# Weight transposes woven into the first chunk's projections, and a narrower wait in the attention loop

## The chip, the cores and the metric

One Trainium2 chip, all 8 cores. Every core runs the same program on its own batch entry (8 entries); the cores exchange nothing. The metric is device microseconds of the slowest core.

## What is computed

For each batch entry x (4096 x 2048, float32), with layernorms that have no weights:

```
q, k, v = LN(x) @ wq.T, LN(x) @ wk.T, LN(x) @ wv.T      # 16 heads of 128, q scaled by 1/sqrt(128)
scores  = einsum('bshd,bstd->bsht', q, k)               # at each position, its 16 heads against each other
out     = softmax(scores) @ v                           # then transposed and reshaped to 4096 x 2048
x = x + LN(out @ wo.T)
ternary(w) = clip(round(w / mean|w|), -1, 1)            # for w1, w2 (5632 x 2048), w3 (2048 x 5632)
x = x + LN((sigmoid(h @ ternary(w1).T) * (h @ ternary(w2).T)) @ ternary(w3).T),   h = LN(x)
```

All weights arrive as float32 with the wrong axis on the partitions, so each is cast (or made ternary) to bf16 and transposed 128 x 128 at a time on TensorE against an identity. The transposed copy is written to HBM and streamed from there.

## The kernel before

The program is one list of instructions for each engine, filled by Python in the order of the code. Each engine works its own list strictly in order. Counters T, V and C count what TensorE (PE), VectorE (DVE) and ScalarE (ACT) have finished. `emit` puts the waits in front of an instruction; `dma` puts a transfer on the list of the engine named (SyncE "sync"/SP, ScalarE "scalar"/ACT, GpSimd "gpsimd"/POOL), so the transfer is not issued before that engine has come to it, and each engine's transfers use four semaphore slots in turn.

**Prelude.** 64 weight tiles (`units`: q, k, v, o, 16 row blocks of 128 each). Per tile: two loads of 128 x 1024 float32 (line 506; the first from SP, the second from POOL; four landing buffers `fwl`), two casts on DVE (line 511) into one of three `wstream` buffers, four groups of four 128 x 128 transposes on PE (line 523) into PSUM banks 2 and 3 in turn, a copy of each group on ACT (line 531) into one of three `tpstage` buffers, and a store of each group from ACT (line 535; for o line 540). A `tpstage` buffer is taken again when its store has landed. `wst_cons[b]` holds the T count at which `wstream[b]` was last read.

**Phase 2, eight chunks of 512 positions (c = 0..7).** Each chunk has:

- projections: 48 steps (q, k, v by 16 heads; gi = 0..47). A step loads one 128 x 2048 bf16 strip from SP (line 619) into `wstream[gi % 3]`, waiting for `wst_cons[gi % 3]`; runs 16 matmuls of 512 columns (line 626) into bank gi % 2; scatters the result on ACT (line 637 for q, 644 for k, 651 for v); and calls `emit_prep_step()`.
- the transpose of V: 16 groups (PE line 664, DVE line 669), a call of `emit_prep_step()` after each.
- the layernorm of the next chunk.
- the attention loop, lines 681 to 785: `a5_stage_a(it)` (scores on PE, maxima on DVE, line 696) and `a5_stage_b(it - 1)` (exponentials on ACT, line 713; reciprocals and a diagonal on DVE, lines 720 and 725; two rounds of matmuls, lines 734 and 749; copies on ACT, line 742, and DVE, line 767), eight iterations with two halves hv each. `emit_prep_light()` is called at the end of each stage b. In iterations 3 and 7 ACT stores half of the chunk's result.

`emit_prep_step()` does one step of the preparation of w1, w2, w3: first the 272 tiles for the means ("gamma", two to a step, so 136 steps; loads from POOL and ACT in turn, line 359, absolute sums on DVE, line 368), then three steps that compute the thresholds, then 272 "quant" steps (one load from POOL, two DVE instructions, two groups of transposes, copies on ACT, line 454, stores from ACT, line 460). `emit_prep_light()` does gamma only. When gamma is done, the light calls do nothing.

After the eight chunks come the output projection and the feed-forward part, which need `woT`, `w1T`, `w2T` and `w3T`.

Of the kernel before, what the change touches and what calls it, by code (L numbers as in the profile page):

```python
# [29 lines left out]
def latest(toks):  # L30
    d = {}
    for c, v in toks:
        k = id(c)
        if k not in d or d[k][1] < v:
            d[k] = (c, v)
    return list(d.values())
# [37 lines left out]
def build_nc(debug=False):  # L74
# [82 lines left out]
    T = _mkctr("T", 1)  # L157
    V = _mkctr("V", 1)
# [38 lines left out]
    def se(waits, build, inc=None):  # L197
        emit("scalar", waits, build, inc)
# [5 lines left out]
    def dma(eng, waits, build):  # L204
        q = QENG[eng]
        slot = q.next_slot()
        emit(eng, list(waits) + [(slot, slot.n)], build, inc=slot, fresh=True)
        return (slot, slot.n)
# [204 lines left out]
    def emit_quant_step():  # L413
        if q_state["i"] >= len(q_tiles):
            return False
        wi, srcw, t, c0, cw = q_tiles[q_state["i"]]
        if not thr_state["done"][wi]:
            return False
        b = q_state["i"] % 2
        q_state["i"] += 1  # L420
        tok = dma("gpsimd", [(V, q_state["cons"][b])],
                  lambda e, d=wload_q[b], s=srcw, t=t, c0=c0, cw=cw:
                  e.dma_start(d[:, 0:cw],
                              s[t * 128:(t + 1) * 128, c0:c0 + cw]))
        fg = q_state["first_gate"]
        q_state["first_gate"] = []
        ve([tok, (V, thr_state["v"][wi])] + fg,
           lambda e, s=wload_q[b], cw=cw, wi=wi: e.tensor_scalar(  # L428
               lbuf[:, 0:cw], s[:, 0:cw], thrn[:, wi:wi + 1], None,
               ALU.is_le), V)  # L430
        ve([(T, q_state["mm"][b])],
           lambda e, s=wload_q[b], q=qstage[b], cw=cw, wi=wi:
           e.scalar_tensor_tensor(q[:, 0:cw], s[:, 0:cw],  # L433
                                  thr[:, wi:wi + 1], lbuf[:, 0:cw],
                                  ALU.is_ge, ALU.subtract), V)
        q_state["cons"][b] = V.n
        stt_v = V.n
        for g in range(cw // 512):
            bank = 2 + q_state["tp"] % 2
            tb = q_state["tp"] % 3  # L440
            q_state["tp"] += 1
            tw = [(V, stt_v)] + (bank_free[bank] or []) + consts_toks
            for i in range(4):
                te(tw if i == 0 else [],
                   lambda e, bk=bank, q=qstage[b], g=g, i=i: e.matmul(  # L445
                       ps[bk][:, i * 128:(i + 1) * 128],
                       q[:, g * 512 + i * 128: g * 512 + (i + 1) * 128],
                       ident, start=True, stop=True),
                   T if i == 3 else None)
            mm = T.n  # L450
            q_state["mm"][b] = mm
            se([(T, mm)] + ([q_state["tp_cons"][tb]]
                            if q_state["tp_cons"][tb] else []),
               lambda e, bk=bank, tb=tb: e.copy(tpstage[tb], ps[bk][:]), C)  # L454
            bank_free[bank] = [(C, C.n)]
            if wi < 2:
                wTd = w1T_h if wi == 0 else w2T_h
                stok = dma("scalar", [(C, C.n)],
                           lambda e, d=wTd, t=t, c0=c0, g=g, tb=tb:
                           e.dma_start(  # L460
                               d[t][:, c0 + g * 512: c0 + (g + 1) * 512],
                               tpstage[tb]))
            else:
                ccb = (c0 + g * 512) // 128
                zoff = (t % 4) * 128
                stok = dma(
                    "scalar", [(C, C.n)],
                    lambda e, t=t, ccb=ccb, zoff=zoff, tb=tb: e.dma_start(
                        w3T_h[t // 4].rearrange("p (cc z) -> p cc z", z=512)[
                            :, ccb:ccb + 4, zoff:zoff + 128],  # L470
                        tpstage[tb].rearrange("p (i z) -> p i z", i=4)))
            q_state["tp_cons"][tb] = stok
            q_state["store_toks"][wi].append(stok)
        return True
# [19 lines left out]
    fwl_cons = [0, 0, 0, 0]  # L494
    fwl_toks = []
    wst_cons = [0, 0, 0]
    wT_gate = {w: {} for w in ("q", "k", "v", "o")}
    units = [(w, t) for w in ("q", "k", "v", "o") for t in range(16)]
    for u, (w, t) in enumerate(units):
        cb_ = u % 3  # L500
        src = win["w" + w] if w != "o" else win["wo"]
        for hf in range(2):
            fb = (2 * u + hf) % 4
            ltok = dma("sync" if hf == 0 else "gpsimd",
                       [(V, fwl_cons[fb])],
                       lambda e, d=fwl[fb], s=src, t=t, hf=hf: e.dma_start(
                           d, s[t * 128:(t + 1) * 128,
                                hf * 1024:(hf + 1) * 1024]))
            fwl_toks.append(ltok)
            ve([ltok, (T, wst_cons[cb_])],  # L510
               lambda e, d=wstream[cb_], s=fwl[fb], hf=hf: e.tensor_copy(
                   d[:, hf * 1024:(hf + 1) * 1024], s), V)
            fwl_cons[fb] = V.n
        cast_v = V.n
        toks = []
        for g in range(4):
            bank = 2 + g % 2
            tb = q_state["tp"] % 3
            q_state["tp"] += 1
            tw = [(V, cast_v)] + (bank_free[bank] or []) + consts_toks  # L520
            for i in range(4):
                te(tw if i == 0 else [],
                   lambda e, bk=bank, s=wstream[cb_], g=g, i=i: e.matmul(  # L523
                       ps[bk][:, i * 128:(i + 1) * 128],
                       s[:, (g * 4 + i) * 128:(g * 4 + i + 1) * 128],
                       ident, start=True, stop=True),
                   T if i == 3 else None)
            mm = T.n
            se([(T, mm)] + ([q_state["tp_cons"][tb]]
                            if q_state["tp_cons"][tb] else []),  # L530
               lambda e, bk=bank, tb=tb: e.copy(tpstage[tb], ps[bk][:]), C)  # L531
            bank_free[bank] = [(C, C.n)]
            if w != "o":
                stok = dma("scalar", [(C, C.n)],
                           lambda e, w=w, t=t, g=g, tb=tb: e.dma_start(
                               wT[w][t][:, g * 512:(g + 1) * 512],
                               tpstage[tb]))
            else:
                stok = dma("scalar", [(C, C.n)],
                           lambda e, t=t, g=g, tb=tb: e.dma_start(  # L540
                               woT_h[4 * g:4 * g + 4][
                                   :, :, t * 128:(t + 1) * 128].rearrange(
                                   "j p c -> p j c"),
                               tpstage[tb].rearrange("p (j c) -> p j c",
                                                     j=4)))
            q_state["tp_cons"][tb] = stok
            toks.append(stok)
        wst_cons[cb_] = T.n
        wT_gate[w][t] = toks
    woT_gate = latest([t for h in range(16) for t in wT_gate["o"][h]])  # L550
    fwl_gate = latest(fwl_toks)
    fcmax = max(fwl_cons)
    q_state["cons"] = [fcmax, fcmax]
    q_state["first_gate"] = fwl_gate

    if NPHASES <= 1:
        ops_end(nc, refs, ops, Q_S, Q_C, Q_G, se, emit)
# [5 lines left out]
    A_half_tok = [[None, None] for _ in range(NCH)]  # L563
    last_exp = [0, 0]
    last_rec = [0, 0]
    nmx_v = [0, 0]
    last_aT_mm = [0, 0]
    last_out_mm = [0, 0]
    ln1T_ready = [None, None]
# [39 lines left out]
    for c in range(NCH):  # L609
# [3 lines left out]
        for pi, p in enumerate(("q", "k", "v")):  # L613
            ename = "scalar"
            for h in range(H):
# [35 lines left out]
                       lambda e, d=dst, s=srcp: e.activation(d, s, ACT.Copy),  # L651
                       C)
                bank_free[bank] = [(ECTR[ename], ECTR[ename].n)]
                emit_prep_step()
        ln1T_cons[par] = T.n
        qkv_done = [(V, V.n), (C, C.n)]

# [20 lines left out]
        def a5_stage_a(it):  # L678
            for hv in range(2):
# [5 lines left out]
                for i in range(4):  # L685
# [10 lines left out]
                   lambda e, b=sbk, d=nm: e.tensor_reduce(  # L696
                       d, ps[b][:].rearrange("p (g cc) -> p g cc", g=4),
                       AX.X, ALU.max, negate=True), V)
                nmx_v[hv] = V.n

        def a5_stage_b(it):
            nonlocal_A = [0]
            for hv in range(2):
# [3 lines left out]
                ex = expS[hv]  # L707
                su = sums4[hv]
                for g in range(4):
                    se([(V, nmx_v[hv]), (T, last_aT_mm[hv]),  # L710
                        (V, last_rec[hv])] if g == 0 else [],
                       lambda e, b=sbk, g=g, ex=ex, nm=nm, su=su:
                       e.activation(ex[:, g * 128:(g + 1) * 128],  # L713
                                    ps[b][:, g * 128:(g + 1) * 128],
                                    ACT.Exp, bias=nm[:, g:g + 1],
                                    accum_out=su[:, g:g + 1]), C)
# [76 lines left out]
    w1T_gate = latest(q_state["store_toks"][0])  # L793
    w2T_gate = latest(q_state["store_toks"][1])
    w3T_gate = latest(q_state["store_toks"][2])

    if NPHASES <= 2:
        ops_end(nc, refs, ops, Q_S, Q_C, Q_G, se, emit)
# [404 lines left out]
```

How the kernel before makes its waits and increments, by code:

```python
        def step(e, ws=ws, build=build, inc=inc):  # L180
            for ctr, val in ws:
                e.wait_ge(ctr.sem, val)
            ins = build(e)
            if inc is not None:
                if ins is None:
                    e.nop().then_inc(inc.sem, inc.step)
                else:
                    ins.then_inc(inc.sem, inc.step)
```

## Time and profile before

| what | us |
| --- | --- |
| median of 5 runs | 10075.22 |
| lowest and highest of them | 9974.32, 10541.44 |
| the profiled execution | 9962.73 |
| its span on core 7, the slowest, read below | 9960.8 |
| spans of the 8 cores in it | 9795.2 to 9960.8 |

A stretch of the trace is given by its start and end in us from the start of the span. The chunks of core 7 were told apart by the first and last start of the matmuls of lines 626, 664 and 749: chunk 0's projections run from 577.0, chunk 1's from 1049.9, chunk 2's from 1480.7, chunk 4's from 2418.9, chunk 6's from 3339.8, chunk 7's from 3672.5, and the output projection begins at 3968.4. PE is busy for 67% of the span, and the other engines for a quarter or less.

### The profile page before, as it was taken

What the parts mean: (1) busy time and instruction counts of PE and PEld (TensorE: products, weight loads), DVE (VectorE), ACT (ScalarE), POOL (GpSimd) and SP (SyncE); (2) the same over time, 40 slices, a digit from 0 to 9 for tenths busy, and PEclk for the clock granted to TensorE, in tenths of its full rate; (3) what the DMA queues carried; (4) which work ended last, traced back from release to release, by engine and by line L of the source; (5) the groups of instructions that cost most, each with busy time, mean ns of one, the idle gap of its engine ahead of it and who ended that gap; (6) DMA issues with size and microseconds to landing.
All of it is one profiled execution on the core that took longest, in us unless ns stands there. A gap on an engine that the chain in (4) does not pass through costs nothing.

```text
span 9960.8 us, 102628 instructions; the slowest of 8 cores (9795.2 to 9960.8 us)
## 1 busy us (share of the span) xinstructions
PE 6637.0 (67%) x30924; PEld 2992.5 (30%) x30924; DVE 2522.0 (25%) x3692; ACT 1956.5 (20%) x3811; POOL 414.7 (4%) x764
## 2 busy tenths in 40 slices
PE   2253637374645666686786786886885885896896
PEld 1121213232323323232332332332332332332342
DVE  1146554444444321202102102102102102102101
ACT  2231224334343442101001001001001001001000
POOL 0000001010000000000000000000000000000000
PEclk9996859586867777798898998998997897786787
DMA  7777858484757532343443443443443443442433
GB/s 210 200 242 222 259 166 248 120 243 132 229 150 206 146 109 87 116 148 113 138 144 108 145 150 104 151 148 103 149 143 99 153 141 99 137 144 93 142 121 108
DMA packets 725709, 1510.76 MB, mean 152 GB/s; under 512 B 316336, under 2 KB 418992, under 8 KB 704688
## 3 DMA queue, kind: packets, MB, share of 16 engines
q1 hardware_dynamic: 300464, 772.17, 24.9%
q10 hardware_dynamic: 340864, 421.61, 13.7%
q0 software_dynamic: 83840, 310.43, 11.0%
q8 instruction: 259, 4.24, 0.2%
q14 instruction: 282, 2.31, 0.1%
HBM read 1283.75 MB, written 203.42 MB: 149 GB/s over the span
## 4 chain that ended last, share of the span: by engine, by line
PE 44%; DMA 26%; DVE 13%; ACT 9%; issue 6%; ACTq 1%; DVEq 1%; SPq 0%; POOLq 0%
PE ps L981 12%; PE ps L990 12%; PE ps L1037 9%; DMA bfar<-w3T 6%; PE ps L626 5%; DMA bfar<-woT 4%; DMA f32ar<-w 4%; PE ps L880 2%; ACT bfar L713 2%; DMA w1T<-bfar 2%; DMA w3T<-bfar 2%; ACT bfar L454 2%; DVE f32ar L368 1%; DVE f32ar L273 1%; DMA w2T<-bfar 1%
## 5 line engine op out<-in xcount | busy, mean ns | idle before, releaser
L1037 PE MATMUL ps<-bfar 128*128 128x512 bf16 x5632 | 1365.8, 405 | 661.6 <-DMA bfar<-w3T 661.2
L626 PE MATMUL ps<-bfar 128*128 128x512 bf16 x6144 | 1437.2, 392 | 160.7 <-DMA bfar<-wT_q 67.5
L981 PE MATMUL ps<-bfar 128*128 128x512 bf16 x5632 | 1357.0, 397 | 232.5 <-ACT f32ar L1000 199.5
L990 PE MATMUL ps<-bfar 128*128 128x512 bf16 x5632 | 1327.9, 391 | 0.0
L1037 PEld LDWEIGHTS ps<-bfar 128*128 128x128 bf16 x5632 | 564.4, 103 | 1459.5 <-issue 1023.5
L626 PEld LDWEIGHTS ps<-bfar 128*128 128x128 bf16 x6144 | 602.4, 100 | 902.1 <-issue 281.2
L981 PEld LDWEIGHTS ps<-bfar 128*128 128x128 bf16 x5632 | 569.0, 101 | 965.6 <-issue 455.5
L1006 DVE TENSOR_TENSOR bfar<-ps,f32ar 128x512 bf16<-128x512 f32 x352 | 243.4, 691 | 2244.6 <-PE ps L990 2222.8
L990 PEld LDWEIGHTS ps<-bfar 128*128 128x128 bf16 x5632 | 563.7, 100 | 706.0 <-issue 178.1
L880 PE MATMUL ps<-bfar 128*128 128x512 bf16 x2048 | 566.5, 427 | 272.8 <-DMA bfar<-woT 223.4
L1000 ACT ACTIVATE f32ar<-ps 128x512 f32<-128x512 f32 x352 | 210.2, 597 | 2210.0 <-PE ps L981 2209.3
L734 PE MATMUL ps<-bfar 128*128 128x128 bf16 x512 | 75.0, 301 | 645.3 <-DVE bfar L725 645.3
L1062 DVE TENSOR_REDUCE f32ar<-bfar 128x1 f32<-128x512 bf16 x128 | 87.8, 686 | 1596.7 <-ACT bfar L1055 1590.1
L445 PE MATMUL ps<-bfar 128*128 128x128 bf16 x2112 | 208.0, 240 | 371.7 <-DVE bfar L433 218.7
L454 ACT CAST bfar<-ps 128x512 bf16<-128x512 f32 x528 | 309.5, 586 | 663.0 <-PE ps L445 300.1
L523 PE MATMUL ps<-bfar 128*128 128x128 bf16 x1024 | 149.7, 300 | 367.7 <-ACT bfar L531 353.2
L880 PEld LDWEIGHTS ps<-bfar 128*128 128x128 bf16 x2048 | 203.4, 105 | 635.6 <-issue 505.7
L368 DVE TENSOR_REDUCE f32ar<-f32ar 128x1 f32<-128x1024 f32 (+1 forms) x269 | 319.6, 1188 | 258.1 <-DMA f32ar<-w 242.6
L433 DVE SCALAR_TENSOR_TENSOR bfar<-bfar,f32ar 128x1024 bf16<-128x1024 f32 (+1 forms) x272 | 340.9, 1253 | 95.6 <-PE ps L445 71.3
L637 ACT ACTIVATE bfar<-ps,f32ar 128x512 bf16<-128x512 f32 x128 | 312.8, 2444 | 225.1 <-PE ps L626 102.9
L1055 ACT CAST bfar<-ps 128x512 bf16<-128x512 f32 x64 | 37.5, 586 | 1550.8 <-PE ps L1037 1548.1
L428 DVE TENSOR_SCALAR bfar<-bfar,f32ar 128x1024 f32<-128x1024 f32 (+1 forms) x272 | 200.7, 738 | 517.0 <-DMA bfar<-w 507.9
(100 smaller groups left out, 3801.5 us busy)
## 6 DMA issues: line engine op xcount, KB each, us to landing
bfar<-w1T SPq DMA_DIRECT2D x352, 512.0 KB, 3.6
bfar<-w2T SPq DMA_DIRECT2D x352, 512.0 KB, 3.7
bfar<-w POOLq DMA_DIRECT2D x256, 512.0 KB, 6.1
bfar<-w3T ACTq DMA_DIRECT2D x192, 512.0 KB
bfar<-w3T SPq DMA_DIRECT2D x160, 512.0 KB, 3.6
f32ar<-w POOLq DMA_DIRECT2D x136, 512.0 KB, 6.7
bfar<-wT_q SPq DMA_DIRECT2D x128, 512.0 KB, 5.6
bfar<-wT_k SPq DMA_DIRECT2D x128, 512.0 KB, 6.4
```

Source lines behind the costliest of these rows:

```text
L368: ve([tok], lambda e, s=wload_g[b], cw=cw, a=acol: e.tensor_reduce(gtmp[:, a + 8:a + 9], s[:, 0:cw], AX.X, ALU.add, apply_absolute_value=T ...
L433: e.scalar_tensor_tensor(q[:, 0:cw], s[:, 0:cw], thr[:, wi:wi + 1], lbuf[:, 0:cw], ALU.is_ge, ALU.subtract), V)
L445: lambda e, bk=bank, q=qstage[b], g=g, i=i: e.matmul(ps[bk][:, i * 128:(i + 1) * 128], q[:, g * 512 + i * 128: g * 512 + (i + 1) * 128], i ...
L454: lambda e, bk=bank, tb=tb: e.copy(tpstage[tb], ps[bk][:]), C)
L626: e.matmul(ps[b][:], wl[:, Dc * 128:(Dc + 1) * 128], lt[:, Dc * 512:(Dc + 1) * 512], start=(Dc == 0), stop=(Dc == 15)),
L637: lambda e, d=dst, s=srcp: e.activation(d, s, ACT.Copy, scale=c_qs), C)
L880: te(tw, lambda e, cbq=cbq, sl=sl, j=j: e.matmul(ps[cbq][:], Aslab[cbq][:, j * 128:(j + 1) * 128], wostrip[sl], start=(j == 0), stop=(j == ...
L981: lambda e, b=b1, s1=s1, lt=lt, Dc=Dc: e.matmul(ps[b][:], wpool[s1][:, Dc * 128:(Dc + 1) * 128], lt[:, Dc * 512:(Dc + 1) * 512], start=(Dc ...
L990: lambda e, b=b2, s2=s2, lt=lt, Dc=Dc: e.matmul(ps[b][:], wpool[s2][:, Dc * 128:(Dc + 1) * 128], lt[:, Dc * 512:(Dc + 1) * 512], start=(Dc ...
L1000: lambda e, b=b1, sg=sg: e.activation(sg, ps[b][:], ACT.Sigmoid), C)
L1006: ve(mw, lambda e, b=b2, cp=cp, sg=sg: e.tensor_tensor(hid[:, cp * 512:(cp + 1) * 512], ps[b][:], sg, ALU.mult), V)
L1037: posb=posb: e.matmul(ps[b][:], hid[:, cc * 512 + posb * 128: cc * 512 + (posb + 1) * 128], wpool[sl][:, ccl * 512:(ccl + 1) * 512], start ...
```

## The change

The prelude keeps its first 16 tiles (q). The body of the prelude's loop becomes `emit_wunit_step()`. The other 48 tiles (k, v, o) are emitted one by one in chunk 0's projections, in place of that chunk's 48 calls of `emit_prep_step()`, each behind the step's scatter. For these 48, the two loads are issued from POOL and ACT instead of SP and POOL. The tile u still goes into `wstream[u % 3]`. What depended on all 64 tiles (first use of the quant buffers, `woT_gate`) is computed where it is needed. In the attention loop, `nmx_v` gets four entries instead of two, so that the exponentials of iteration it wait for the maxima of iteration it, not for those of it + 1.

```diff
--- before.py
+++ after.py
@@ -416,6 +416,11 @@
         wi, srcw, t, c0, cw = q_tiles[q_state["i"]]
         if not thr_state["done"][wi]:
             return False
+        if q_state["i"] == 0:
+            assert wunit_state["i"] == len(units)
+            fcmax = max(fwl_cons)
+            q_state["cons"] = [fcmax, fcmax]
+            q_state["first_gate"] = latest(fwl_toks)
         b = q_state["i"] % 2
         q_state["i"] += 1
         tok = dma("gpsimd", [(V, q_state["cons"][b])],
@@ -496,13 +501,21 @@
     wst_cons = [0, 0, 0]
     wT_gate = {w: {} for w in ("q", "k", "v", "o")}
     units = [(w, t) for w in ("q", "k", "v", "o") for t in range(16)]
-    for u, (w, t) in enumerate(units):
+    wunit_state = {"i": 0}
+
+    def emit_wunit_step():
+        u = wunit_state["i"]
+        if u >= len(units):
+            return False
+        wunit_state["i"] += 1
+        w, t = units[u]
+        woven = u >= 16
         cb_ = u % 3
-        src = win["w" + w] if w != "o" else win["wo"]
+        src = win["w" + w]
         for hf in range(2):
             fb = (2 * u + hf) % 4
-            ltok = dma("sync" if hf == 0 else "gpsimd",
-                       [(V, fwl_cons[fb])],
+            eng = (("gpsimd", "scalar") if woven else ("sync", "gpsimd"))[hf]
+            ltok = dma(eng, [(V, fwl_cons[fb])],
                        lambda e, d=fwl[fb], s=src, t=t, hf=hf: e.dma_start(
                            d, s[t * 128:(t + 1) * 128,
                                 hf * 1024:(hf + 1) * 1024]))
@@ -547,11 +560,10 @@
             toks.append(stok)
         wst_cons[cb_] = T.n
         wT_gate[w][t] = toks
-    woT_gate = latest([t for h in range(16) for t in wT_gate["o"][h]])
-    fwl_gate = latest(fwl_toks)
-    fcmax = max(fwl_cons)
-    q_state["cons"] = [fcmax, fcmax]
-    q_state["first_gate"] = fwl_gate
+        return True
+
+    for _ in range(16):
+        emit_wunit_step()
 
     if NPHASES <= 1:
         ops_end(nc, refs, ops, Q_S, Q_C, Q_G, se, emit)
@@ -563,7 +575,7 @@
     A_half_tok = [[None, None] for _ in range(NCH)]
     last_exp = [0, 0]
     last_rec = [0, 0]
-    nmx_v = [0, 0]
+    nmx_v = [0, 0, 0, 0]
     last_aT_mm = [0, 0]
     last_out_mm = [0, 0]
     ln1T_ready = [None, None]
@@ -651,7 +663,10 @@
                        lambda e, d=dst, s=srcp: e.activation(d, s, ACT.Copy),
                        C)
                 bank_free[bank] = [(ECTR[ename], ECTR[ename].n)]
-                emit_prep_step()
+                if c == 0:
+                    emit_wunit_step()
+                else:
+                    emit_prep_step()
         ln1T_cons[par] = T.n
         qkv_done = [(V, V.n), (C, C.n)]
 
@@ -696,7 +711,7 @@
                    lambda e, b=sbk, d=nm: e.tensor_reduce(
                        d, ps[b][:].rearrange("p (g cc) -> p g cc", g=4),
                        AX.X, ALU.max, negate=True), V)
-                nmx_v[hv] = V.n
+                nmx_v[2 * (it % 2) + hv] = V.n
 
         def a5_stage_b(it):
             nonlocal_A = [0]
@@ -707,7 +722,7 @@
                 ex = expS[hv]
                 su = sums4[hv]
                 for g in range(4):
-                    se([(V, nmx_v[hv]), (T, last_aT_mm[hv]),
+                    se([(V, nmx_v[2 * (it % 2) + hv]), (T, last_aT_mm[hv]),
                         (V, last_rec[hv])] if g == 0 else [],
                        lambda e, b=sbk, g=g, ex=ex, nm=nm, su=su:
                        e.activation(ex[:, g * 128:(g + 1) * 128],
@@ -793,6 +808,7 @@
     w1T_gate = latest(q_state["store_toks"][0])
     w2T_gate = latest(q_state["store_toks"][1])
     w3T_gate = latest(q_state["store_toks"][2])
+    woT_gate = latest([t for h in range(16) for t in wT_gate["o"][h]])
 
     if NPHASES <= 2:
         ops_end(nc, refs, ops, Q_S, Q_C, Q_G, se, emit)
```

## Rows read from the trace of the kernel before

**Rows 1.** The page: busy us (share) xcount of each engine; the chain by engine

```profile
PE 6637.0 (67%) x30924; PEld 2992.5 (30%) x30924; DVE 2522.0 (25%) x3692; ACT 1956.5 (20%) x3811; POOL 414.7 (4%) x764
...
PE 44%; DMA 26%; DVE 13%; ACT 9%; issue 6%; ACTq 1%; DVEq 1%; SPq 0%; POOLq 0%
```

**Rows 2.** Stretches, core 7: start:end, length, busy us (count), granted clock, DMA share, GB/s

```profile
137.40:517.00 379.60, 112.39 (x771) 66.80 (x770) 66.25 (x94) 112.55 (x192) 24.24 (x46) 1.00 0.75 197
...
576.90:813.30 236.40, 184.11 (x768) 75.47 (x768) 117.20 (x170) 56.65 (x46) 22.17 (x42) 0.96 0.94 299
...
931.20:1049.80 118.60, 28.17 (x184) 17.66 (x184) 53.40 (x100) 36.33 (x135) 3.69 (x7) 0.50 0.37 99
...
1049.80:1276.80 227.00, 178.97 (x770) 74.46 (x768) 118.45 (x178) 56.64 (x46) 23.22 (x44) 0.96 0.97 315
...
1389.80:1480.60 90.80, 28.18 (x184) 17.66 (x184) 34.09 (x72) 36.32 (x135) 0.00 (x0) 0.50 0.19 48
...
1727.50:1817.00 89.50, 24.14 (x184) 17.08 (x184) 40.94 (x45) 17.58 (x30) 7.91 (x15) 0.51 0.44 129
...
2418.80:2664.00 245.20, 203.27 (x1146) 99.12 (x1145) 98.64 (x98) 112.98 (x141) 26.14 (x48) 0.94 0.89 261
...
2418.80:2885.90 467.10, 260.48 (x1546) 136.91 (x1544) 193.58 (x236) 187.81 (x374) 34.61 (x64) 0.74 0.64 183
...
3339.70:3672.50 332.80, 219.30 (x1177) 107.65 (x1176) 100.31 (x146) 133.93 (x282) 9.39 (x17) 0.79 0.49 146
...
3533.90:3546.30 12.40, 7.70 (x64) 4.80 (x64) 10.22 (x15) 3.19 (x11) 0.00 (x0) 0.70 0.00 0
...
3672.50:3839.90 167.40, 167.37 (x770) 75.41 (x768) 0.85 (x2) 57.35 (x47) 0.00 (x0) 0.99 0.45 148
```

**Rows 3.** In order of time (start, us), core 7: a weight tile of the prelude

```profile
138.00 1.49 DVE L511 CAST bfar<-bfar 128x1024 bf16<-128x1024 f32 x2 [7.96 <-PE ps L523]
...
138.90 0.59 ACT L531 CAST bfar<-ps 128x512 bf16<-128x512 f32 x1 [0.61 <-ACT bfar L531]
...
139.62 0.33 ACTq L535 DMA_DIRECT2D wT_q<-bfar  x1
...
139.63 0.58 PE L523 MATMUL ps<-bfar 128*128 128x128 bf16 x4 [0.61 <-ACT bfar L531]
...
140.09 0.59 ACT L531 CAST bfar<-ps 128x512 bf16<-128x512 f32 x1 [0.61 <-DMA wT_q<-bfar]
```

**Rows 4.** In order of time, core 7, chunk 0's projections

```profile
583.64 2.43 ACT L637 ACTIVATE bfar<-ps,f32ar 128x512 bf16<-128x512 f32 x1 [37.40 <-PE ps L626]
...
586.14 0.35 ACTq L359 DMA_DIRECT2D f32ar<-w  x1
...
603.25 5.30 PE L626 MATMUL ps<-bfar 128*128 128x512 bf16 x16 [2.29 <-DMA bfar<-wT_q]
...
609.07 3.61 PE L626 MATMUL ps<-bfar 128*128 128x512 bf16 x16 [0.52 <-DMA bfar<-wT_q]
```

**Rows 5.** Transfers: line 506's and the last chunk's strips, us from issue to landing

```profile
DMA to landing us min/median/max: 4.1/6.3/13.1
...
bfar<-wT_k SPq DMA_DIRECT2D x16, 512.0 KB, 3.4
```

**Rows 6.** Line 644, the scatter of a K strip: forms, duration

```profile
L644 ACT ACTIVATE bfar<-ps x128: 597/597/598, 662.1 to 3784.8; 128x512 bf16<-128x512 f32 x128
```

**Rows 7.** In order of time, core 7, the attention loop of the last chunk

```profile
3891.78 0.59 ACT L742 CAST bfar<-ps 128x512 bf16<-128x512 f32 x1 [2.02 <-PE ps L734]
...
3894.33 1.49 DVE L696 TENSOR_REDUCE f32ar<-ps 128x4 f32<-128x512 f32 x2
...
3895.17 0.37 ACT L713 ACTIVATE bfar<-ps,f32ar 128x128 bf16<-128x128 f32 x1 [2.80 <-DVE f32ar L696]
...
3897.09 0.19 ACT L713 ACTIVATION_READ_ACCUMULATOR bfar<-ps,f32ar 128x1 f32 x1
...
3897.46 0.18 DVE L720 RECIPROCAL f32ar<-f32ar 128x4 f32<-128x4 f32 x1 [1.64 <-ACT bfar L713]
```

## The prediction

> **What bounds the kernel now.** I read the page first. Its chain of waits belongs to PE for 44%, to transfers for 26% and to DVE for 13% [rows 1], so no single engine is the limit, and each stage has to be read alone. The stretches of core 7 [rows 2] divide the part that the change touches:
>
> - The part of the prelude for the 48 tiles of k, v and o is 137.4 to 517.0, 379.6 us or 7.9 us a tile, with PE busy for 112 us (771 matmuls against 48 x 16 = 768) and the transfers for 75% of the time.
> - Chunk 0's projections take 236.4 us with transfers busy for 94% at 299 GB/s. The same 768 matmuls take 167.4 us in chunk 7, where nothing is woven in. So the gamma loads set chunk 0's pace: 4.9 us a step against 3.5.
> - Chunk 1's projections (gamma in each step) take 227.0 us, 4.73 a step. Chunk 4's (quant in each) take 245.2, 5.1 a step.
> - The attention loop takes 90.8 us without gamma (chunk 1) and 118.6 with it (chunk 0).
>
> The change takes 48 tiles out of a stage that does nothing else, and puts them under matmuls. The question is what one of the 48 steps costs afterwards.
>
> **Removed.** The prelude ends 379.6 us earlier. The layernorm of chunk 0 behind it is unchanged. Chunk 0's projections in their present form, 236.4 us, go too. Together -616.
>
> **Added: 48 steps of matmuls plus tile.** I follow the lists of the engines. At step gi, the strip is in `wstream[gi % 3]` and the tile u = 16 + gi goes into `wstream[(16 + gi) % 3]`, which is `wstream[(gi + 1) % 3]`: exactly the buffer of the next strip. The load of strip gi + 1 therefore waits until the tile's last transposes have read that buffer. Before, a strip was loaded up to two steps ahead; now none is. The second wait is on ACT: the tile's second load stands on ACT's list behind the scatter of step gi, which waits for the matmuls of step gi. So one step is a chain without overlap:
>
> - 16 matmuls. After an idle time of 2.29 us a group of 16 took 5.30 us, and one that PE entered after only 0.52 us took 3.61 [rows 4]. At the lower of the clock's two levels throughout (512 columns at 1.2 GHz are 0.427 us) it would be 6.8. The two waits of a step are longer than 2.29 us, so I take 6.6, near that end. Bounds: 3.6 and 7.0.
> - Scatter on ACT: 2.43 us for q [rows 4], 0.60 for k and v [rows 6]. With 0.15 for the hand-overs from PE and to the load's issue (586.07 to 586.14 is one of them, [rows 4]) 0.75, for q 2.6.
> - ACT's load of 512 KB. In the prelude such loads landed after 6.3 us in the median, 4.1 at least; strips of the same size in chunk 7, where the transfers are busy for 45% of the time, after 3.4 [rows 2, 5]. Here it shares the 16 transfer engines with little, so I take 3.7. Bounds 3.4 and 6.3.
> - The cast of that half: two took 1.49 us [rows 3], so 0.75, with hand-overs 0.95.
> - Four groups of transposes. PE needs 0.58 a group and starts the third and the fourth 0.14 us after ACT has copied the first and the second; ACT's copies are 1.2 us apart (0.59 for the copy, the rest the store's issue) [rows 3]. So 0.58 + 0.15 + 0.59 + 0.61 + 0.59 + 0.14 + 0.58 = 3.24. The fourth copy also waits for the first store, but PE does not need it, and the ACT list is free long before the next scatter.
> - The strip. It lands beside the tile's stores and POOL's load of a tile ahead, so I take 4.5 rather than 3.4 (bounds 3.4 and 6.3); with 0.2 for hand-overs 4.7.
>
> Sum for k and v: 6.6 + 0.75 + 3.7 + 0.95 + 3.24 + 4.7 = 19.9 us; for q 21.8. 16 x 21.8 + 32 x 19.94 = 987 us. Nothing hides it: PE's list has no other work in this stage. With all lower bounds a step is 15.5 (q 17.4): 775. With all upper bounds 24.7 (q 26.5): 1214.
>
> On the clock, the Trainium skill ("TensorE: Matmul & The Clock Gate", section "HAM oscillation — how this bites in real kernels") says that groups of matmuls with a wait for data between them fall back to the lower clock, each group anew. By that rule every one of the 48 groups would take 16 x 0.427 = 6.8, some 10 us more in all than I take. This trace agrees in kind: the stretches where PE waits often show a granted clock of 0.50, those with dense matmuls 0.94 to 0.99 [rows 2].
>
> **Moved: gamma.** 48 of its 136 steps are displaced. Counting calls (64 `prep_step` a chunk, 8 light): chunk 0 now does 24 gamma steps, chunk 1 72, chunk 2 the last 40, then 3 thresholds and 21 quant; chunks 3 to 5 64 each; 59 are left for chunk 6, which does 19 now. Chunk 7 stays free, so nothing spills behind the chunks.
>
> - Chunk 1's attention loop now carries gamma: 118.6 - 90.8 = +28.
> - Chunk 2: 40 steps at gamma's 4.73 instead of quant's 5.1: -15.
> - Chunk 6 becomes nearly a chunk 4 (467.1 us with 64 quant steps). Five steps fewer in the V transposes, at (89.5 - 12.4) / 16 = 4.8 each, make 443, against 332.8 now [rows 2]: +110.
>
> Together +123. Moving gamma out of chunk 0 is thus no gain; it is paid later, under matmuls that were partly free.
>
> **The narrower wait.** In the loop the exponentials of iteration it start at 3895.17, released by the first of two maxima of it + 1 that run from 3894.33 to 3895.82, though ACT had ended its last copy at 3892.37; they end at 3897.28, and the reciprocal starts at 3897.46 [rows 7]. With the new counts ACT starts about 3892.5 and ends about 3894.6. But the reciprocal stands behind both maxima on DVE's list, so it starts at 3895.9 at the earliest: 1.5 us gained, not 2.7. The last iteration has no later maxima, and the one behind the store in iteration 3 waits on ACT for that store. Six of eight gain: 6 x 1.5 x 8 chunks = 74 us. Bounds: 0 (the store's wait or gamma behind the loop takes it) and 2.7 x 7 x 8 = 151.
>
> **Sum.** 9962.7 - 616 + 987 + 123 - 74 = 10,383, that is +420 on the profiled execution. That execution is 112 us below the median of the runs shown, and I add the +420 to that median: 10,490 us, rounded.
>
> **Rivals.**
>
> - *Hidden after all (the other side).* If strips and the second load were still prefetched, a step would cost PE's own 6.6 + 3.24 = 9.8 at most, or with a warm clock the 7.9 of a prelude tile: 48 x 7.9 = 379, and the sum is 9,775 (9,887 on the median). It decides below (616 - 123 + 74) / 48 = 11.8 us a step. For it: PE and transfers together would have room. Against it: the buffer numbers and the place on ACT's list are in the code, and my lowest step is 15.5. Chance 0.06.
> - *Only one wait is real.* If ACT's load were early, a step would be 6.6 + 3.24 + 4.7 = 14.6, 698 us in all, and the sum 10,094 (+1.3%). Against it: ACT's list is in order, as the load at 586.14 right behind the scatter's end at 586.07 shows [rows 4]. If besides a wait were cheaper than the rows say, the result would be within 1%. Chance 0.08 for all of this, 0.05 of it within 1%.
> - *Transfers as slow as in the prelude.* A step is 24.7, all 1214 us, the sum 10,610, on the median 10,720. For it: the strip lands next to four stores, and those of o are in short pieces. Against it: the transfers would carry 2 MB in 20 us, 100 GB/s, against 197 in the prelude. Chance 0.10.
>
> **How the numbers follow.** The forecast (serial steps of 16 to 23 us) has 0.76, the slow transfers 0.10, one wait 0.08, hidden 0.06. Range: with the lower bounds of the steps the result is 212 us lower (10,280), with the upper ones 228 us higher (10,720); the profiled execution being 112 us under the median lowers the lower end a little. 10,230 to 10,730. A measurement of this kernel can hardly tell less than 1% from no change. Faster by over 1%: 0.06; within 1%: 0.05; slower by over 1%: 0.89.
>
> **What would show it.** In the new trace: 16 tiles of line 523's kind before chunk 0, whose projections begin near 197; then a stretch of some 990 us in which PE waits twice a step, once for a cast (its cause ACT's load) and once for the strip, with the granted clock near 0.5 and transfers near 100 GB/s; strips issued right after a tile's last transposes. Attention loops of 82 us rather than 90.8. Chunk 6 about 110 us longer, the feed-forward part unchanged. I am wrong if strips are issued ahead, if a step is under 12 us, or if the displaced gamma costs nothing.

## The result, and the profile after

| | before | after |
| --- | --- | --- |
| median of all runs, us | 10263.66 (10 runs) | 10526.53 (6 runs) |
| the profiled execution, us | 9962.73 | 10371.89 |
| ratio, with its 95% interval | 1 | 1.0358 (1.0244 to 1.0473) |

The changed kernel is 3.6% slower. In some executions of either kernel the cores of one die or of both show a lower clock and take some per cent longer; the ratio and its interval leave these executions out, and the medians do not. The two profiled executions are 409 us apart.

The slowest core of the profile after is core 3 (before it was core 7). Its page divides the chain nearly as before [rows 1], so the page alone does not show where the time went.

```profile
PE 6684.7 (64%) x30924; PEld 3006.4 (29%) x30924; DVE 2523.1 (24%) x3692; ACT 1953.2 (19%) x3811; POOL 414.7 (4%) x764
...
PE 43%; DMA 28%; DVE 14%; ACT 8%; issue 6%; ACTq 1%; DVEq 1%; SPq 0%; POOLq 0%
```

The stretches show it. Columns as in [rows 2]: start:end, length, busy us of PE, PEld, DVE, ACT and POOL, granted clock, DMA share, GB/s. The rows are the q, k and v steps of chunk 0's projections, the attention loop of chunk 2, and chunk 6 whole.

```profile
195.40:538.30 342.90, 126.05 (x512) 55.48 (x512) 22.21 (x32) 74.88 (x79) 8.45 (x16) 0.63 0.30 94
538.30:867.10 328.80, 130.75 (x512) 56.41 (x512) 22.22 (x32) 47.05 (x81) 8.44 (x16) 0.58 0.34 103
867.10:1184.80 317.70, 128.09 (x495) 55.03 (x496) 20.82 (x30) 44.88 (x77) 7.90 (x15) 0.59 0.40 110
...
2241.70:2326.20 84.50, 28.85 (x189) 18.05 (x190) 34.22 (x73) 36.88 (x136) 0.00 (x0) 0.50 0.22 56
...
3703.80:4120.90 417.10, 250.31 (x1475) 129.30 (x1474) 177.03 (x226) 177.02 (x356) 31.07 (x57) 0.76 0.67 186
```

Chunk 0's projections now take 342.9 + 328.8 + 317.7 = 989.4 us, against 236.4, and neither PE (385 us busy) nor the transfers (a third of the time) are near a limit. That is a stage of waits. From the first matmul of one step to that of the next it is 21.7 us in the q steps and 20.5 in the k and v steps. One k step in order of time (core 3; the first column is the start, the second the duration):

```profile
646.65 5.94 PE L638 MATMUL ps<-bfar 128*128 128x512 bf16 x16 [5.23 <-DMA bfar<-wT_k]
652.68 0.60 ACT L656 ACTIVATE bfar<-ps 128x512 bf16<-128x512 f32 x1 [8.01 <-PE ps L638]
653.36 0.34 ACTq L519 DMA_DIRECT2D bfar<-wv  x1
657.68 1.49 DVE L524 CAST bfar<-bfar 128x1024 bf16<-128x1024 f32 x2 [18.96 <-DMA bfar<-wv]
658.63 1.01 PE L536 MATMUL ps<-bfar 128*128 128x128 bf16 x8 [6.05 <-DVE bfar L524]
...
661.29 0.59 PE L536 MATMUL ps<-bfar 128*128 128x128 bf16 x4 [0.61 <-ACT bfar L544]
...
662.21 0.32 SPq L631 DMA_DIRECT2D bfar<-wT_k  x1
...
666.76 6.12 PE L638 MATMUL ps<-bfar 128*128 128x512 bf16 x16 [4.89 <-DMA bfar<-wT_k]
```

Each link follows the one above it; between the two rows of transposes, and not shown, lie ACT's copies and the third group. PE waits twice: 6.05 us for the cast (line 524), which waits for the load that ACT could only issue at 653.36, behind its scatter; and 4.89 us for the strip, which SP issued at 662.21, when the tile's last transposes had ended at 661.88. The cast row holds two casts, this tile's second half and the next tile's first, whose load POOL had brought long before; PE goes on after the first of them.

### The profile page after: what moved, and what is told of

Same layout as the page of the kernel before. It is cut to its first block, busy times and chain, and to the rows that moved or that the text cites. A ratio compares the mean times of both kernels' runs of the same rounds, so it can differ in the third digit from the quotient of the medians.

```text
span 10370.3 us, 102724 instructions; the slowest of 8 cores (10232.5 to 10370.3 us)
## 1 busy us (share of the span) xinstructions
PE 6684.7 (64%) x30924; PEld 3006.4 (29%) x30924; DVE 2523.1 (24%) x3692; ACT 1953.2 (19%) x3811; POOL 414.7 (4%) x764
## 4 chain that ended last, share of the span: by engine, by line
PE 43%; DMA 28%; DVE 14%; ACT 8%; issue 6%; ACTq 1%; DVEq 1%; SPq 0%; POOLq 0%
PE ps L997 12%; PE ps L1006 11%; PE ps L1053 8%; DMA bfar<-w3T 6%; PE ps L638 6%; DMA bfar<-woT 4%; DMA f32ar<-w 4%; DMA w2T<-bfar 2%; PE ps L896 2%; DMA bfar<-w 2%; DVE f32ar L273 1%; DVE f32ar L368 1%; ACT bfar L728 1%; DVE bfar L438 1%; ACT bfar L459 1%
## 5 line engine op out<-in xcount | busy, mean ns | idle before, releaser
L459 ACT CAST bfar<-ps 128x512 bf16<-128x512 f32 x528 | 308.9, 585 | 707.9 <-PE ps L450 341.1
L524 DVE CAST bfar<-bfar 128x1024 bf16<-128x1024 f32 x128 | 88.8, 694 | 1055.8 <-DMA bfar<-wk 344.3
```

## The experiments

The ratios are to repeats of the kernel before that were run beside each kernel. Stage lengths are read from the trace of the core named, and where it is said so they are means over several cores. "Phase 2 ends" means the start of the last matmul of chunk 7's attention loop, counted from the start of the span. On the mean of the eight cores that is 3937 us in the kernel before and 4387 in the changed one.

### The tile in another buffer

```diff
-        cb_ = u % 3
+        cb_ = (u + 2) % 3 if woven else u % 3
```

> The changed kernel with one edit: a woven tile uses the wstream buffer of the strip that has just been multiplied, not that of the next strip. ACT still issues the tile's second load. Theory (a serial chain of two waits, in which the strip's load is one link): strips are again issued ahead, PE's wait for a strip goes, and a step of chunk 0 loses that link of about 4.9 us: 6.1 (matmuls) + 0.75 + 4.2 + 0.95 + 3.25 + 0.2 = 15.5 us for k and v, 17.3 for q, 773 us for the 48 steps against 989, so about 216 us less than the changed kernel. Rival (the transfers themselves, their sum or the ring of three staging buffers, set the 20.6 us): the stage stays within 5% of 989 us.

### The loads from SP and POOL

```diff
-            eng = (("gpsimd", "scalar") if woven else ("sync", "gpsimd"))[hf]
+            eng = ("sync", "gpsimd")[hf]
```

> The changed kernel with one edit: the woven tiles' loads are issued from SP and POOL, as in the prelude, so none stands behind the scatter on ACT. The buffer of the tile is still that of the next strip. Theory: scatter, ACT's load and the cast leave the chain: 6.1 + 3.25 + 4.9 + 0.2 = 14.4 us a step, the same for q as for k and v, 693 us for the stage, about 297 less than the changed kernel. Rival (transfers set the step): within 5% of 989 us. A second rival, that a load costs more on SP because SP waits there for the strip's buffer: between 693 and 989, with casts that wait for SP's load.

The stage rows of both, first the rotated buffer (core 1):

```profile
198.30:940.50 742.20, 352.04 (x1520) 164.82 (x1520) 65.23 (x94) 167.34 (x235) 25.31 (x48) 0.69 0.46 136
```

then the loads from SP and POOL (core 3):

```profile
192.80:870.00 677.20, 328.45 (x1520) 143.05 (x1521) 66.62 (x96) 167.02 (x235) 25.30 (x48) 0.73 0.49 150
```

989 became 742 us with the one edit (773 expected) and 677 with the other (693 expected). The means of the eight cores are 991, 740 and 675. The waits of PE in the stage, in us in total, times and longest, separate the two links. In the changed kernel (core 3) there are both kinds; the wait of 59.3 us in the q row is that for chunk 0's first strip, before the stage:

```profile
PE ps L536 <- DVE bfar L524: 304.2, 47, 7.7
...
PE ps L638 <- DMA bfar<-wT_q: 139.1, 16, 59.3
PE ps L638 <- DMA bfar<-wT_v: 85.0, 16, 7.7
PE ps L638 <- DMA bfar<-wT_k: 84.2, 16, 5.8
```

With the rotated buffer the wait for strips is gone but for the very first, and the wait for casts stays:

```profile
PE ps L536 <- DVE bfar L524: 338.8, 47, 14.4
...
PE ps L638 <- DMA bfar<-wT_q: 58.4, 1, 58.4
```

With the loads from SP and POOL it is the other way round: the wait for strips stays, and the one for casts no longer appears in the list:

```profile
PE ps L638 <- DMA bfar<-wT_q: 128.6, 16, 58.4
PE ps L638 <- DMA bfar<-wT_v: 80.9, 16, 6.3
PE ps L638 <- DMA bfar<-wT_k: 79.8, 16, 5.8
```

So each of the two edits of the code owns one wait, and both waits are needed for a step of some 21 us. The rival, that the transfers themselves set the pace, falls: the same transfers went through at 136 and 150 GB/s instead of about 100. The second rival of the SP loads, casts that wait for SP's load, falls too as far as PE is concerned, since PE waits for no cast.

### Both edits together

The two diffs above in one kernel.

> The changed kernel with both edits: the tile in the buffer of the strip just multiplied, and its loads from SP and POOL. Theory: no transfer is left in the chain; what remains is matmuls, two casts (the buffer is free only after the matmuls) and the transposes: 5.8 + 1.7 + 3.25 = 10.7 us at the lower clock level, 8.5 if the clock is at the upper one; I expect 9.5, 456 us for the stage, some 530 less than the changed kernel, which makes this kernel about 1% faster than the one before. Rival (transfers set the step): about 2 MB a step at the 299 GB/s that chunk 0 had before would be 7 us, so no limit here; if contention were the cause, the stage would stay above 700 us.

```profile
200.30:675.00 474.70, 295.21 (x1496) 135.13 (x1518) 66.20 (x96) 168.18 (x236) 25.31 (x48) 0.84 0.73 214
```

475 us (core 6), 456 expected. Single gains of 247 and 312 us add up to 559; together they gave 515. Against the kernel before the ratio is 0.9943 (0.9766 to 1.012), which by itself leaves open whether it is faster. The traces say that it is: phase 2 ends at 3852 us on the mean of the eight cores, 85 earlier than in the kernel before, and the part behind it is not changed by the edits. The granted clock of the stage rose from about 0.60 to 0.84, and PE is busy for 298 us (core 3, also a stage of 475 us) instead of 385 with the same matmuls. So 87 of the 515 us are the faster clock. It followed from the waits here, since nothing in these edits touches PE's work, but it is part of what removing them gave.

### Buffers of their own for the tiles

```diff
+    ubuf = [BF[:, 72832 + i * 2048: 72832 + (i + 1) * 2048]
+            for i in range(2)]
+    ub_cons = [0, 0]
...
-        cb_ = u % 3
+        cb_ = u % 2
...
-            ve([ltok, (T, wst_cons[cb_])],
-               lambda e, d=wstream[cb_], s=fwl[fb], hf=hf: e.tensor_copy(
+            ve([ltok, (T, ub_cons[cb_])],
+               lambda e, d=ubuf[cb_], s=fwl[fb], hf=hf: e.tensor_copy(
...
-                   lambda e, bk=bank, s=wstream[cb_], g=g, i=i: e.matmul(
+                   lambda e, bk=bank, s=ubuf[cb_], g=g, i=i: e.matmul(
...
-        wst_cons[cb_] = T.n
+        ub_cons[cb_] = T.n
...
-            eng = (("gpsimd", "scalar") if woven else ("sync", "gpsimd"))[hf]
+            eng = ("sync", "gpsimd")[hf]
```

> As the kernel with both edits, but the tiles have two buffers of their own in unused memory and leave wstream to the strips, so the casts run ahead too. Theory: a step is the larger of PE's own time (matmuls 3.5 to 5.8 plus transposes 3.25) and the 7.9 us that the ring of three staging buffers allows a tile: 8 to 9 us, about 405 us for the stage, 50 less than with the shared buffer, and 1.5 to 2% faster than the kernel before. Rival (the shared buffer was no limit once strips are early): no difference to the kernel with both edits.

```profile
192.90:665.10 472.20, 289.05 (x1519) 136.64 (x1520) 66.61 (x96) 167.27 (x235) 25.30 (x48) 0.83 0.76 215
```

472 us on core 3, where the mean of cores 0 to 3 is 465 and was 475 with both edits: 11 us less. I expected 405 us, so this is a miss, and the rival named there was nearly right. What took its place can be read from PE's waits before the transposes. With both edits (core 3, in the stage) PE waits for casts and for ACT's copies:

```profile
PE ps L536 <- DVE bfar L524: 85.4, 44, 2.3
PE ps L536 <- ACT bfar L544: 85.1, 96, 6.6
```

With own buffers (core 3) the wait for casts is gone from the list, and the wait for copies has grown by about as much:

```profile
PE ps L539 <- ACT bfar L547: 183.1, 119, 6.4
```

The copies in turn wait for staging buffers: ACT stands 165 us in the stage, 59 times, for stores to land (135 us with both edits; two rows of a k step, core 3):

```profile
413.12 0.59 ACT L547 CAST bfar<-ps 128x512 bf16<-128x512 f32 x1 [3.05 <-DMA wT_v<-bfar]
...
413.85 0.58 PE L539 MATMUL ps<-bfar 128*128 128x128 bf16 x4 [3.26 <-ACT bfar L547]
```

ACT stands 3.05 us for a store before it can copy a group, and PE, in order, waits 3.26 us behind it for the bank. Not every such wait costs PE its full length: one of 5.74 us at 406.45 lay under PE's matmuls and cost it 0.57. There is no ratio to the kernel before for this kernel. In the profiled execution cores 0 to 3 took 9691 to 9718 us, where those of the kernel before took 9795 to 9819.

### A longer ring

```diff
-    tpstage = [BF[:, 71808:72320], BF[:, 72320:72832], BF[:, 77952:78464]]
+    tpstage = [BF[:, 71808:72320], BF[:, 72320:72832], BF[:, 77952:78464],
+               BF[:, 76928:77440], BF[:, 77440:77952]]
...
-    Q_C = Queue("dC")
+    Q_C = Queue("dC", 8)
```

on top of the kernel with own buffers.

> The kernel with own buffers for the tiles and loads from SP and POOL, and besides five staging buffers instead of three and eight semaphore slots for ACT's transfers instead of four. Theory: the 7.9 us of a tile in the prelude are the round trip of a staging buffer (four groups over three buffers), so the 16 tiles that stay in the prelude take about 6.2 us each (-27 us), the woven steps about 7.5 (-25 to -60), quant steps may gain a little: 60 to 90 us less than with own buffers alone, about 2.5% faster than the kernel before. Rival (a tile is limited by the bandwidth, busy for 75%): no gain over the kernel with own buffers.

The prelude's 16 tiles without this edit, with it, and the stage with it (all core 3):

```profile
14.40:133.70 119.30, 35.95 (x248) 21.46 (x248) 22.26 (x31) 35.81 (x61) 7.92 (x15) 1.00 0.70 214
...
14.40:113.70 99.30, 36.07 (x248) 21.54 (x248) 21.87 (x30) 35.75 (x61) 7.92 (x15) 1.00 0.87 257
173.10:591.80 418.70, 268.86 (x1519) 131.47 (x1520) 66.60 (x96) 167.07 (x235) 25.32 (x48) 0.87 0.84 242
```

A tile of the prelude takes 99.3 / 16 = 6.2 us instead of 119.3 / 16 = 7.5, 20 us for the 16 tiles where 27 were expected. So the waits for stores were the limit, and the rival, a limit by bandwidth, falls: the same tiles moved at 257 GB/s instead of 214. The edit changes two things, the buffers and the semaphore slots, and they were not tried apart; with three buffers no more than three stores can be outstanding, so the four slots were not yet in the way.

The stage is 419 us, 53 less. ACT waits for stores 33 us instead of 165, and PE for copies 150 instead of 183. The rest is the clock: the same matmuls keep PE busy for 269 us instead of 289, at a granted clock of 0.87 instead of 0.83. On the mean of cores 0 to 3 phase 2 ends 95 us earlier than with own buffers alone (60 to 90 expected): 21 in the prelude, 52 in the stage, and the rest in later chunks, whose quant steps share the ring.

This kernel is faster than both: the ratio to the kernel before is 0.9767 (0.9632 to 0.9901), and its cores took 9591 to 9645 us in the profiled execution, where those of the changed kernel took 10233 to 10370. Of the 2.3%, 0.8% is the narrower wait (below). A q step still takes 9.9 us where a k step takes 7.3 (from the starts of their first matmuls), and the rows say why:

```profile
258.68 0.61 PE L541 MATMUL ps<-bfar 128*128 128x128 bf16 x8
258.94 2.40 ACT L654 ACTIVATE bfar<-ps,f32ar 128x512 bf16<-128x512 f32 x1 [3.37 <-PE ps L643]
...
261.42 0.59 ACT L549 CAST bfar<-ps 128x512 bf16<-128x512 f32 x1
...
262.15 0.38 PE L541 MATMUL ps<-bfar 128*128 128x128 bf16 x4 [2.86 <-ACT bfar L549]
...
263.57 5.30 PE L643 MATMUL ps<-bfar 128*128 128x512 bf16 x16
```

The copy that frees the third group's bank stands behind q's scatter of 2.40 us on ACT, PE waits 2.86 us for it, and the next 16 matmuls take 5.30 us, much as after the 2.29 us of idle time in [rows 4]. That four banks instead of two would remove this was not tried.

### The narrower wait alone

```diff
-    nmx_v = [0, 0]
+    nmx_v = [0, 0, 0, 0]
...
-                nmx_v[hv] = V.n
+                nmx_v[2 * (it % 2) + hv] = V.n
...
-                    se([(V, nmx_v[hv]), (T, last_aT_mm[hv]),
+                    se([(V, nmx_v[2 * (it % 2) + hv]), (T, last_aT_mm[hv]),
```

in the kernel before.

> The kernel before with only the narrower wait of the attention loop (four entries in nmx_v). Theory: the reciprocal stays behind the later maxima on DVE's list, so an iteration gains 1.5 us, not the 2.7 that ACT waited: attention loops of 82 instead of 90.6 us, with the first iteration's gain in front of them some 80 us in all, 0.8% faster. Rival (the whole wait is gained): loops of about 72 us, 150 us in all, 1.5% faster. Second rival (the gain is taken back by gamma or by the next chunk's layernorm): no change.

The attention loop of chunk 2 (core 1):

```profile
1816.00:1898.10 82.10, 28.01 (x183) 17.51 (x184) 34.10 (x72) 36.20 (x135) 0.00 (x0) 0.50 0.22 56
```

82.1 us, and 90.3 in the kernel before. From chunk 0's first projection to the last loop's end it is 3292 us (core 1) against 3373 on core 3 and 3376 on core 7 of the kernel before: 81 to 84 us less, 80 expected. The means of cores 0 to 3 are 3285 and 3365, also 80 less. The ratio is 0.9851 (0.9729 to 0.9974), faster, with a centre beyond what the trace accounts for but an interval that holds the 0.8%. Why the gain is 1.5 us an iteration and not 2.7 is to be seen in the changed kernel's loop (core 3, last chunk):

```profile
4314.63 0.58 ACT L757 CAST bfar<-ps 128x512 bf16<-128x512 f32 x1 [2.02 <-PE ps L749]
4315.31 0.37 ACT L728 ACTIVATE bfar<-ps,f32ar 128x128 bf16<-128x128 f32 x1
...
4317.18 1.49 DVE L711 TENSOR_REDUCE f32ar<-ps 128x4 f32<-128x512 f32 x2
...
4318.76 0.18 DVE L735 RECIPROCAL f32ar<-f32ar 128x4 f32<-128x4 f32 x1
```

ACT starts its exponentials at once and has ended them at 4317.41, but the reciprocal stands on DVE's list behind the maxima, which end at 4318.67. From the end of ACT's copy to the reciprocal it is 3.55 us; in [rows 7] it was 5.09. That is 1.54 us.

### The displaced gamma alone

```diff
-                emit_prep_step()
+                if c > 0:
+                    emit_prep_step()
```

in the projections of the kernel before.

> The kernel before, with its whole prelude, in which only chunk 0's projections call no preparation step; the 48 gamma steps move to later chunks, as in the changed kernel. Theory: chunk 0's projections fall from 236 to about 167 us (-69), and the displaced steps cost about +123 later (attention loop of chunk 1 +28, chunk 2 -15, chunk 6 +110): together +54 us, 0.5% slower. Rival (displaced work is absorbed in steps with room): -69 us, 0.7% faster.

Chunk 0's projections, chunk 0 whole, and the rest up to the end of the last attention loop (core 2):

```profile
566.30:734.20 167.90, 167.88 (x767) 75.66 (x768) 0.00 (x0) 57.31 (x47) 0.00 (x0) 1.00 0.45 157
566.30:956.50 390.20, 209.17 (x1040) 101.06 (x1040) 127.21 (x197) 113.38 (x248) 12.17 (x23) 0.72 0.48 152
956.50:3981.00 3024.50, 1707.23 (x9406) 857.14 (x9404) 1283.99 (x1747) 1087.93 (x2208) 205.04 (x383) 0.75 0.62 186
```

The same two stretches of the kernel before (core 7):

```profile
577.00:1049.90 472.90, 226.07 (x1041) 101.41 (x1042) 258.19 (x387) 113.31 (x248) 36.95 (x70) 0.74 0.74 231
1049.90:3953.20 2903.30, 1689.01 (x9405) 853.06 (x9404) 1151.79 (x1556) 1089.13 (x2208) 179.93 (x335) 0.75 0.59 176
```

Chunk 0 gains 83 us (69 of them in the projections, as expected; behind them the V transposes begin after 1.3 us and no longer after 18.7) and the later chunks pay 121. The net is +38 us between these two cores, +54 expected. The means of cores 0 to 3 of both kernels are 81 gained and 127 paid, a net of +46, and these cores took 9828 to 9873 us where those of the kernel before took 9795 to 9819. The rival, that displaced work disappears in steps with room, falls. There is no ratio for this kernel, so the size rests on the traces.

## Why the prediction was right

The prediction was 10,490 us, and the median is 10526.53. The sum made for the profiled execution was 10,383, and the profiled execution after took 10371.89. The mechanism, two waits that make a step serial, is shown by the first two experiments, and the size of every term by the traces. That the totals came out so close is partly luck, as the end of this section shows. Step by step, for a k step (the rows above):

| link | predicted | measured |
| --- | --- | --- |
| 16 matmuls, to the scatter's start | 6.6 + 0.08 | 652.68 - 646.65 = 6.03 |
| scatter, to the load's issue | 0.67 | 653.36 - 652.68 = 0.68 |
| ACT's load | 3.7 | 657.68 - 653.36 = 4.32 |
| cast | 0.95 | 658.63 - 657.68 = 0.95 |
| four groups of transposes | 3.24 | 661.88 - 658.63 = 3.25 |
| strip | 4.7 | 666.76 - 661.88 = 4.88 |
| step | 19.94 | 20.11 |

Two errors cancelled. The matmuls were 0.6 us faster than I took them, and the transfers slower by 0.6 and 0.2. Over the 48 groups the first and the last start lay 5.5 us apart on average on core 3 (5.6 on core 1), where the lower level throughout would make 15 x 0.427 = 6.4. In each of the 48 groups on core 3 the first two matmuls start 0.38 us apart and the next 0.43, which is the lower level, and the last two 0.22 to 0.26, which is the upper; 6 to 14 of the 15 intervals are long. The granted clock of the stage is accordingly 0.58 to 0.63, not near the 0.5 that I named.

The Trainium skill ("TensorE: Matmul & The Clock Gate", section "HAM oscillation — how this bites in real kernels") says that each group after a wait for data starts at the lower clock. This trace agrees: 48 of 48 groups started there. They did not stay there to their end, and my 6.6 us supposed that they nearly would.

The stage's 989.4 us end at the last step's matmuls. My 987 were for 48 whole steps, and these end with the last tile's transposes, 1002 us after the first matmul, when the transpose of V begins. The sum is hardly hurt, since what I took out, the old 236.4, was cut in the same way and had 18.7 us behind it where the new stage has 12.5.

Two readings in the prediction were not right, and neither moved the sum much. Six times 1.5 times 8 is 72; the 74 comes from an unrounded 1.54. And the sentence that stretches where PE waits often show a granted clock of 0.50 leaves out the prelude's row in [rows 2], which shows 1.00 with PE busy for 112 of 379.6 us. That 1.00 is not borne out by the matmuls: a group of four transposes takes 0.58 us there [rows 3], as it does in the k step above, and 0.38 in the stage of the kernel with the long ring. The trace of core 7 holds no record of the clock before 583.0 us, so the number says nothing about the prelude.

The terms, by the first matmul of each chunk, as means of the eight cores (chunk 7 up to the last matmul of its attention loop; the narrower wait is counted with 9 us a chunk; rounded):

| stretch | before | after | change | predicted |
| --- | --- | --- | --- | --- |
| up to chunk 0's projections | 564 | 195 | -369 | -380 |
| chunk 0's projections, first to last matmul | 236 | 991 | +756 | +751 |
| the rest of chunk 0 | 238 | 225 | -13 | -9 |
| chunk 1 | 431 | 465 | +34 | +19 |
| chunk 2 | 467 | 451 | -17 | -24 |
| chunks 3 to 5 | 1386 | 1373 | -13 | -28 |
| chunk 6 | 334 | 414 | +81 | +101 |
| chunk 7 | 282 | 272 | -10 | -9 |
| all | 3937 | 4387 | +450 | +421 |

- *Prelude.* Chunk 0's projections begin at 195 us. Before, they began at 577.0 on core 7, the core that I read, but at 564 on the mean of the cores and at 559 on core 3. So 382 us are gone by core 7, and 369 on average.
- *Narrower wait.* 80 us by the experiment alone, 74 predicted. Six of eight iterations gain, as I said: in the last chunk on core 3, counted by the first score matmuls, six are shorter by 1.5 to 1.8 us, the one behind the store by nothing (13.40 and 13.36 us), and the loop by 9.6 in all instead of the 9.2 that I took. In the changed kernel chunks 3 to 5 gained only 13 us together, where the experiment's gained 32 by the means of cores 0 to 3. Of the difference 10 us are the displaced gamma, which alone makes these three chunks 10 us longer. For the rest I have no cause; their projections also differ from core to core within one kernel (235.5 and 248.9 us in chunk 4 of the changed kernel, cores 0 and 3).
- *Displaced gamma.* 121 to 127 us by the experiment, 123 predicted. Inside the term there were two errors. Chunk 6 pays less: 417.1 us against 332.8, which with the 10 us of the narrower wait added back is +94, not +110. And chunk 1's projections, which I took to stay at 227.0, took 241.6 us in the changed kernel and 244 with the displaced gamma alone. The gamma tiles that chunk 1 reads are others than before: w3's tiles, one in six of them half as wide, had fallen into chunk 1 and now fall mostly into chunk 2. That accounts for a part only: the stretch moves 302 GB/s x 241.6 us = 73.0 MB where it moved 315 x 227.0 = 71.5, 2% more or 5 of the 15 us. The rest stays open.

So the effect up to the end of phase 2 is +450 us on average, and I had predicted +420. Between core 7 before (3953) and core 3 after (4393), the slowest of the two profiled executions, it is +440. That these differ by only 409 in all is because the part behind phase 2, where the edits do nothing, was not the same on the slowest cores: before it took 6007 us on core 7 and 5887 on core 3, after it took 5977 on core 3 and 5835 to 5875 on cores 0, 1, 4 and 5. The slowest core's time carries 100 us or more in both executions that no term of the change describes. That this extra was 30 us less after hid most of my error. Nor does the median confirm much: 10526.53 lies halfway between two executions of 10371.89 and 10681.16 us, and the median before rose from the 10075.22 that I started from to 10263.66 with five more runs. The ratio of 1.0358 is 357 us on 9962.73; +450 and +420 lie within its interval (243 to 471).

The rival of transfers as slow as in the prelude falls by the rows of the k step (4.32 and 4.88 us, 100 GB/s). The v steps, in which the tiles of o are stored in short pieces, took 20.5 us like the k steps.

The rival on the other side, the hidden tiles, had its turning point at 11.8 us a step. The kernels of the experiments lie on both sides of it. With both edits a step takes 9.9 us, so phase 2 should end 92 us earlier than in the kernel before, and it ends 85 earlier; with the loads from SP and POOL a step takes 14.1, so it should end 110 us later, and it ends 120 later. The turning point was about right too.

What the experiments leave open: whether weaving is worth anything once it is repaired. The longer ring speeds up the prelude as well. By the rows, 48 tiles in a prelude with the longer ring would take 48 x 6.2 = 298 us and chunk 0's projections with gamma 236, together 534; woven they take 419, and the displaced gamma costs 121 to 127, together 540 to 546. That is an estimate from these rows, not shown: the kernel with the long ring and nothing woven was not run.

## What to carry to other kernels

When work is woven into a loop, look first at what it shares with the loop: a buffer ring indexed by the loop's own counter, and the place of every wait and transfer on each in-order list. One shared index and one load behind one evacuation turned a step that could take 10 us into one of 21. And count what the new work pushes out: it has to be paid in another stage, and whether that stage has room is read from its own row, not from the average.

## What the runs showed that I had not expected

- Removing a wait moves the limit to the next ring. After strips, loads and buffers were all early, ACT still stood 165 us of the stage for stores of 128 KB to land. Two more staging buffers (with more semaphore slots) gave 53 us in the stage and 1.2 us on each tile of the prelude.
- Two unequal fixes were nearly additive (247 and 312 us alone, 515 of 559 together), because each owned a link of one serial chain. The third fix, own buffers, gave 11 us: it removed PE's wait for casts (85 us on core 3), and the wait for copies grew from 85 to 183.
- Shorter waits also gave a faster clock, and the same matmuls in the stage cost less: PE was busy for 385 us in the changed kernel, 298 with both edits and 269 with the longer ring, at granted clocks of about 0.60, 0.84 and 0.87.
- A wait of 2.86 us in the middle of a step was followed by 16 matmuls in 5.30 us, although PE had been busy just before it. In a k step of the same kernel, where the waits were 1.06 and 1.33 us, they took 3.62:

```profile
405.02 0.38 PE L541 MATMUL ps<-bfar 128*128 128x128 bf16 x4 [1.33 <-ACT bfar L549]
405.24 3.62 PE L643 MATMUL ps<-bfar 128*128 128x512 bf16 x16
```
